# Early-fusion transformer on one core: when VectorE copies turned weights in the elastic attention, and how the expert weights are folded

## Chip, cores and metric

One NeuronCore of a Trainium2 chip runs the whole network in one launch. The metric is the device time in microseconds of one execution. All data are f32 in this part of the kernel; a matmul of f32 is issued as two passes, so that the trace shows two weight loads and two matmul records for each.

## What is computed

16 samples have 141 tokens each (64 image patches and 77 text tokens) of 192 features. A patch embedding is followed by two layers. The change touches the first layer's feed-forward block, which has an attention of its own, and a preparation for the second layer's experts.

```python
# first layer, "ffn": x [16, 141, 192]; large half (samples 0-7) and small half (8-15)
nl, ns = ln(x[:8]), ln(x[8:])
attn(xp, keep): q, k, v of 12 heads of 16; softmax(q k^T * scale) v; @ w_proj + b_proj
x = x + concat(attn(nl, all heads), sum_i gumbel[i] * attn(ns, 12 / (1, 2, 3) heads))
x = x + mlp(ln(x)), the small half with three widths of the input (192, 96, 64 features)

# second layer, attention of 4 experts
for e in range(4):
    o_e = windowed_attention_e(x)            # 12 heads of 16
    outs.append(o_e @ wo[e].T)
fused = concat(outs)
gate, value = silu(fused @ w_gate.T), fused @ w_up.T
```

Since nothing stands between `wo[e]` and the gate and up weights, the kernel multiplies them together once: for each expert a product of 192 x 192 by 192 x 384, called the fold.

## The kernel before, in words

The work is written out by hand for each engine. Every engine has its own program, run in order, and waits on semaphores. TensorE multiplies and turns, VectorE and ScalarE read its results out of the eight PSUM banks, GpSimd (POOL) scales the softmax weights and normalises tiles, SyncE issues DMAs.

**Elastic attention** (the loops `for n in range(B + 2)` of the four engines, B = 16). Iteration n scores sample n and finishes sample n - 1. TensorE's order in iteration n is: turn groups 0 and 1 of sample n - 1 (L1258), the scores of sample n into banks 0 to 3 (L1244) and of the 13 tail tokens of all heads into bank 7 (L1251), turn groups 2 and 3 (L1258), the V product of sample n into bank 6 (L1232), turn groups 4 and 5 (L1258), turn the tail rows (L1266), the output product of sample n - 2 (L1294), transposes of finished tiles (L700 to L706), the attended values of sample n - 1 (L1279), the q and k products of sample n + 2 (L505). A group is the softmax weights of four heads for one half of the keys, turned; the even groups go through bank 4 and the odd ones through bank 5, so that group u waits until group u - 2 has been copied out. ScalarE copies groups 0, 1 and 4 (L1370), VectorE groups 2, 3 and 5 (L1446).

ScalarE's order in iteration n is: copies of groups 0 and 1, the k copies (L497, L499), exponentials of bank 0, of the tail and of bank 1 (L1389, L1396), the copy of group 4, the tail copies (L1378, L1381), exponentials of banks 2 and 3, the evacuation of a turned tile (L711, L714). Each exponential is recorded as two instructions. Exponentials wait for the negated maxima that VectorE takes: L1425 for bank 0 and for bank 1, L1432 for the tail, and L1435 for banks 2 and 3 in one instruction.

VectorE's order in iteration n is: q of sample n + 1 (L482 to L489), `maxima(n)` with L1425, L1432, L1425, L1435, copies of groups 2 and 3 (L1446), copies of V (L1453), reciprocals of the sums (L1441, L1485), the copy of group 5, a residual addition, more reciprocals, the finish of sample n - 2 (L1468), statistics, and the copies of the attended values (L1462). POOL multiplies the weights by the reciprocals (L1506, L1519) for the turns of the next iteration.

**Fold.** It stands in the MLP block, between the first layer's first up product and the second: `up(0)`, `fold_products`, `up(1)`, `wide_down(0)`, and so on. `up_all(g)` (L1532) multiplies 384 tokens into banks 0 to 5, first six matmuls of 128 rows, then six of 64 rows that lie in the upper and the lower half of the array in turn; ScalarE's gelus (L1650) empty the banks. `fold_products` (L568) makes two products for each expert, of 128 and of 64 output rows, each from a chunk of 128 and a chunk of 64 contracted rows. They go to banks 6 and 7 in turn; ScalarE copies each out (L577, L580) into `gu_w0` and `gu_w1`. `up(1)` waits for all eight copies in its middle, ahead of three forward transposes (L705, L706) into banks 6 and 7, whose inputs POOL makes (L695). POOL then adds the residual tiles (L1725, L1728).

**Loads.** `load_late` on SyncE loads the weights of the MLP and of the fold once the first normalisation is through, and then waits (L552's issues) until the first attention has ended before it loads the experts' weights. The fold's inputs lie in a buffer of hidden values that is not used before the second up product.

Of the kernel before, what the change touches and what calls it, by code (L numbers as in the profile page):

```python
# [24 lines left out]
P = 128  # L25
C = 192
C1 = C - P
# [10 lines left out]
NH, HD, HP = 12, 16, 32  # L38
HB = NH // 4
EXPERTS = 4  # L40
# [21 lines left out]
def fusion_kernel(nc: bass.Bass, d: dict, out: bass.AP):  # L62
    with ExitStack() as ctx:
# [477 lines left out]
        def load_late(sp):  # L541
# [3 lines left out]
            for e in range(EXPERTS):  # L545
                sp.dma_start(eo[:, e, :, :].rearrange("p c (h x) -> p (c h) x", x=HD),
                             d["e_o"][e].rearrange("p c (h x) -> p (c h) x", x=HP)[:, :, 0:HD]).then_inc(w_fold, 16)
            sp.dma_start(eg[:, :, :], d["e_gu"].rearrange("e p c n -> p e (c n)")).then_inc(w_fold, 16)
# [10 lines left out]

        def fold_products(pe):  # L560
            pe.wait_ge(w_fold, 16 * (EXPERTS + 1))
            for e in range(EXPERTS):
                for b, rows_b in CH:
                    u = e * 2 + b
                    if u >= 2:
                        pe.wait_ge(s_c, u - 1)
                    for c, n in CH:
                        mm = nc.tensor.matmul(bank[6 + u % 2][0:rows_b, 0:2 * C],  # L568
                                              eo[0:n, e, c, b * P:b * P + rows_b],
                                              eg[0:n, e, c * 2 * C:(c + 1) * 2 * C],  # L570
                                              start=(c == 0), stop=(c == 1))
                    mm.then_inc(s_f, 1)

        def fold_evacuate(act):
            for e in range(EXPERTS):
                act.wait_ge(s_f, 2 * e + 1)
                nc.scalar.copy(gu_w0[:, e, :], bank[6][:, 0:2 * C]).then_inc(s_c, 1)  # L577
                act.wait_ge(s_f, 2 * e + 2)
                lo = e % 2 * C1
                nc.scalar.copy(gu_w1[lo:lo + C1, e // 2, :], bank[7][0:C1, 0:2 * C]).then_inc(s_c, 1)  # L580
# [27 lines left out]
        with ExitStack() as ph:  # L608
# [204 lines left out]
            with nc.Block() as block:  # L813
# [609 lines left out]
                def _(dve):  # L1423
# [4 lines left out]
                    def maxima(n):  # L1428
# [5 lines left out]
                        maximum(1)  # L1434
                        nc.vector.tensor_reduce(MX[:, 6:12].rearrange("p (i x) -> p i x", i=2),  # L1435
# [36 lines left out]
                    for n in range(B + 2):  # L1472
# [9 lines left out]
                        if n < B:  # L1482
                            evacuate_v(n)
# [45 lines left out]
                def _(pe):  # L1529
# [6 lines left out]
                    def up_all(g):  # L1536

                        pe.wait_ge(s_nev, T3 + min(3 * g + 3, IN_F))
                        for m in range(HM):
                            if m_first[g] + m >= 6:  # L1540
                                pe.wait_ge(s_mgl, m_first[g] + m - 5)
                            elif m == 4:
                                pe.wait_ge(s_nra, T3 + BACK_F)
                                pe.wait_ge(s_nev, T3 + IN_F)
                                pe.wait_ge(sf_o, 2 * B)
                            up_part(g, m, m, 0, 0, P, True, False)
# [822 lines left out]
```

## Time and profile before

| | us |
|---|---|
| median of 3 runs | 1101.53 (1101.25 to 1103.44) |
| the profiled execution | 1101.19 |
| its span, first to last instruction | 1099.5 |
| TensorE busy | 1062.5 |
| ScalarE busy | 763.4 |
| VectorE busy | 722.5 |
| POOL busy | 570.6 |

The span is what the trace sees; 1.7 us of the execution lie around it. Times in the rows are from the span's start. PE is a matmul on TensorE, PEld a weight load, DVE is VectorE, ACT is ScalarE, SP is SyncE. A row of a timeline gives the start, the duration, the engine, the line, the operation, output and input and the count; in brackets stands how long the engine was idle before it and which instruction of another engine ended that ("issue": none that the trace shows). Ends of matmuls are modelled, so a merged group may seem to overlap the next by 0.1 us.

### The profile page before, as it was taken

The page shows a single profiled execution, that of the slowest core. Times are in us where ns is not written, and L with a number is a line of the kernel's source. Part 1 is how long each engine was busy: PE and PEld are TensorE (multiplying, and loading weights), DVE is VectorE, ACT ScalarE, POOL GpSimd, SP SyncE. Part 2 cuts the span into 40 slices and gives each one's busy share as a digit, 9 for nine tenths or more (in the row PEclk, how much of TensorE's full clock was granted, in tenths as well). Part 3 has the DMA queues.
Part 4 walks back from the last instruction along what each step waited for, and adds up shares of the span by engine and source line. Part 5 has one row for each costly group of instructions (what it writes and reads, how often), then busy time and mean ns, then how long its engine had stood idle before and what let it go on. Part 6 is the DMA issues. An engine that isn't in the chain of part 4 may idle for free.

```text
span 1099.5 us, 34055 instructions
## 1 busy us (share of the span) xinstructions
PE 1062.5 (97%) x13103; PEld 864.5 (79%) x13103; DVE 722.5 (66%) x2256; ACT 763.4 (69%) x3370; POOL 570.6 (52%) x859
## 2 busy tenths in 40 slices
PE   6999998999999999999999999999999999999998
PEld 4788886777777475358888888888888888888677
DVE  8666567667766214367888878887888888887201
ACT  2356557777777435549988889888888888888231
POOL 2156766454455677436655465564465565566200
PEclk9999999999999999999999999999999999999999
DMA  8100603000000000010000000000000000000001
GB/s 275 30 6 1 137 2 76 6 2 1 2 1 1 1 1 1 1 52 3 2 3 3 3 2 3 3 3 3 3 2 2 3 2 3 3 2 3 11 22 33
DMA packets 35056, 19.66 MB, mean 18 GB/s; under 512 B 24656, under 2 KB 32336, under 8 KB 34896
## 3 DMA queue, kind: packets, MB, share of 16 engines
q1 hardware_dynamic: 34752, 17.00, 5.9%
q8 instruction: 105, 1.72, 0.7%
q14 instruction: 55, 0.45, 0.1%
q10 hardware_dynamic: 144, 0.49, 0.1%
HBM read 14.93 MB, written 1.77 MB: 15 GB/s over the span
## 4 chain that ended last, share of the span: by engine, by line
PE 89%; DVE 6%; ACT 3%; issue 1%; POOL 1%; DMA 1%; SPq 0%; DVEq 0%; POOLq 0%
PE banks L1750 8%; PE banks L1821 8%; PE banks L1758 6%; PE banks L1837 5%; PE banks L1532 5%; PE banks L1809 4%; PE banks L1856 4%; PE banks L2202 3%; PE banks L2156 3%; PE banks L1814 3%; PE banks L1258 2%; PE banks L505 2%; PE banks L1861 2%; PE banks L1279 2%; PE banks L1797 2%; PE banks L1844 2%
## 5 line engine op out<-in xcount | busy, mean ns | idle before, releaser
L2123 POOL TENSOR_TENSOR e_W<-e_W,e_RS 128x384 f32<-128x384 f32 x256 | 205.2, 828 | 231.7 <-DVE e_RS L1997 229.6
L1947 ACT ACTIVATE e_W<-banks,e_MX 128x128 f32<-128x128 f32 x768 | 270.1, 371 | 16.7 <-DVE e_MX L1983 16.6
L1947 ACT ACTIVATION_READ_ACCUMULATOR e_W<-banks,e_MX 128x1 f32 x768 | 161.2, 210 | 0.0
L1750 PE MATMUL banks<-XT,e_wqk 64*128 64x141 f32 x744 | 119.2, 295 | 0.0
L1750 PEld LDWEIGHTS banks<-XT,e_wqk 64*128 64x128 f32 x744 | 96.3, 188 | 18.1 <-issue 16.6
L1758 PE MATMUL banks<-e_wv,XT 128*128 128x192 f32 (+3 forms) x512 | 109.9, 344 | 0.6 <-DVE e_PT L2001 0.6
L1821 PE MATMUL banks<-ident,e_W 128*128 128x128 f32 x768 | 105.5, 273 | 1.2 <-POOL e_W L2123 0.8
L1506 POOL TENSOR_TENSOR f_W<-f_W,e_RS 128x423 f32<-128x423 f32 x64 | 56.3, 892 | 86.8 <-DVE e_RST L1485 76.5
L1941 ACT COPY e_PT<-banks 128x512 f32<-128x512 f32 x128 | 68.8, 589 | 40.5 <-PE banks L1821 40.3
L1983 DVE TENSOR_REDUCE e_MX<-banks 128x3 f32<-128x384 f32 x128 | 65.4, 552 | 40.1 <-PE banks L1809 40.1
L1821 PEld LDWEIGHTS banks<-ident,e_W 128*128 128x128 f32 x768 | 87.2, 143 | 2.4 <-DVE e_V L2010 1.0
L1758 PEld LDWEIGHTS banks<-e_wv,XT 128*128 128x128 f32 (+3 forms) x512 | 72.1, 166 | 4.6 <-DVE e_PT L2001 0.8
L1389 ACT ACTIVATE f_W<-banks,e_MX 128x141 f32<-128x141 f32 x192 | 70.2, 394 | 2.7 <-DVE e_MX L1425 2.0
L1837 PE MATMUL banks<-e_PT,e_V 128*32 128x128 f32 x1536 | 68.7, 277 | 0.0
L1809 PE MATMUL banks<-e_K,e_Q 32*128 32x128 f32 x1536 | 62.4, 285 | 0.0
L1258 PE MATMUL banks<-ident,f_W 128*70 128x128 f32 (+1 forms) x384 | 51.6, 276 | 10.3 <-DVE f_PT L1446 8.0
L1650 ACT ACTIVATE m_hid<-banks,vecs 128x384 f32<-128x384 f32 x72 | 38.1, 580 | 33.3 <-PE banks L1532 33.3
L1532 PE MATMUL banks<-XT,m_w 128*128 128x384 f32 (+1 forms) x216 | 60.8, 512 | 0.0
L1989 DVE TENSOR_REDUCE e_MX<-banks 128x6 f32<-128x768 f32 x64 | 60.6, 948 | 0.0
L1837 PEld LDWEIGHTS banks<-e_PT,e_V 128*32 128x32 f32 x1536 | 51.6, 109 | 9.2 <-issue 0.5
L1856 PE MATMUL banks<-e_ON,e_guw 128*128 128x141 f32 x384 | 57.9, 287 | 0.3 <-DVE e_ON L2022 0.3
L1258 PEld LDWEIGHTS banks<-ident,f_W 128*70 128x70 f32 (+1 forms) x384 | 40.7, 128 | 18.2 <-issue 14.9
(328 smaller groups left out, 2716.1 us busy)
## 6 DMA issues: line engine op xcount, KB each, us to landing
xp<-in_patches_dram SPq DMA_DIRECT2D x4, 768.0 KB, 9.3
H<-in_h_dram SPq DMA_DIRECT2D x1, 1728.0 KB, 13.4
out_dram<-H SPq DMA_DIRECT2D x6, 288.0 KB, 2.3
m_hid<-in_e_gu_dram SPq DMA_DIRECT2D x1, 1536.0 KB, 8.4
m_hid<-in_e_o_dram SPq DMA_DIRECT2D x4, 192.0 KB, 6.9
e_wqk<-in_e_qk_dram SPq DMA_DIRECT2D x8, 96.0 KB, 2.4
e_wqk<-in_e_qk_dram SPq DMA_DIRECT2D x24, 32.0 KB, 2.3
tokw<-in_tok_w_dram SPq DMA_DIRECT2D x1, 576.0 KB, 5.3
```

What stands on the lines that cost most here:

```text
L1258: tr = nc.tensor.transpose(bank[4 + u % 2][0:nk, x * P:(x + 1) * P], f_W[n % 2][:, u // 2 * 4 + x, k0:k0 + nk], ident[:, :])
L1389: ex = nc.scalar.activation(f_W[n % 2][:, t, :], bank[i][:, x * SEQ:(x + 1) * SEQ], ACT.Exp, bias=MX[:, t:t + 1], accum_out=SM[n % 2][:, t ...
L1532: return nc.tensor.matmul(bank[u % 6][:, 0:GT_], m_w1[lo:lo + n, c, m * P:(m + 1) * P], XT[lo:lo + n, c, g * GT_:(g + 1) * GT_], start=sta ...
L1750: return nc.tensor.matmul(bank[6][:, m * SEQ:(m + 1) * SEQ], ew[n % EXPERTS][0][0:rows_c, c, m * P:(m + 1) * P], XT[0:rows_c, c, tokens(n) ...
L1758: return nc.tensor.matmul(bank[4][0:nk, i * C:(i + 1) * C], XT[lo:P, c, at:at + nk], ew[n % EXPERTS][1][lo:P, c, :], start=start, stop=sto ...
L1809: mm = nc.tensor.matmul(bank[i][:, x * P:(x + 1) * P], QE[n % 2][HP * i:HP * (i + 1), q, :], KM[n % 2][HP * i:HP * (i + 1), k, 0:P], start ...
L1821: tr = nc.tensor.transpose(dst[:, (t % 4) * P:(t % 4 + 1) * P], W[n % 2][:, t, :], ident[:, :])
L1837: nc.tensor.matmul(bank[5][HP * c:HP * (c + 1), col:col + P], VP[n % 2][:, 0, h, :], PT[:, slot_of[h], :], start=(c not in seen), stop=(h ...
L1856: mm = nc.tensor.matmul(bank[7][:, m * SEQ:(m + 1) * SEQ], gu_w0[:, e, m * P:(m + 1) * P], ON[:, 0, :], start=(e == 0 and m == 0), stop=False,
L1941: nc.scalar.copy(PT[:, 4 * u:4 * u + 4, :], bank[4 + u][:, 0:4 * P]).then_inc(s_pa, 1)
L1947: ex = nc.scalar.activation(W[n % 2][:, t, :], bank[i][:, x * P:(x + 1) * P], ACT.Exp, bias=MX[:, t:t + 1], accum_out=SM[n % 2][:, t:t + 1])
L2123: nc.gpsimd.tensor_tensor(x, x, RS[n % 2][:, 3 * i:3 * i + 3].unsqueeze(2).broadcast_to([P, 3, P]), ALU.mult).then_inc(s_nm, 1)
```

## The change

In the elastic attention `maxima(n)` loses its last reduction, which becomes `last_maxima()` and is called behind the copies of groups 2 and 3 and ahead of the V copies. In the fold two experts are treated at once. The 64-row chunk of an odd expert is loaded to partitions 64 to 127, and its products of 64 output rows are written to partitions 64 to 127, so that the four kinds of product are issued in pairs: two full ones, two in the row halves, two in the column halves, two on the diagonal. The eight results have a bank each, of which banks 0 to 5 need the gelus' semaphore; `up_all(1)` waits for the copies bank by bank. Five DMAs become sixteen, which leave the padding out.

```diff
@@ load_late
             for e in range(EXPERTS):
-                sp.dma_start(eo[:, e, :, :].rearrange("p c (h x) -> p (c h) x", x=HD),
-                             d["e_o"][e].rearrange("p c (h x) -> p (c h) x", x=HP)[:, :, 0:HD]).then_inc(w_fold, 16)
-            sp.dma_start(eg[:, :, :], d["e_gu"].rearrange("e p c n -> p e (c n)")).then_inc(w_fold, 16)
+                lo = e % 2 * C1
+                for c, at, n in ((0, 0, P), (1, lo, C1)):
+                    sp.dma_start(eo[at:at + n, e, c, :].rearrange("p (h x) -> p h x", x=HD),
+                                 d["e_o"][e][0:n, c, :].rearrange("p (h x) -> p h x", x=HP)[:, :, 0:HD]).then_inc(w_fold, 16)
+                    sp.dma_start(eg[at:at + n, e, c * 2 * C:(c + 1) * 2 * C], d["e_gu"][e][0:n, c, :]).then_inc(w_fold, 16)
@@ the fold
+        FOLD_BANKS = ((6, 7, 0, 1), (2, 3, 4, 5))
+
+        def fold_part(dst, e, c, b, rows_b, start, stop):
+            lo, n = (e % 2 * C1, C1) if c else (0, P)
+            at = e % 2 * C1 if b else 0
+            return nc.tensor.matmul(dst[at:at + rows_b, 0:2 * C], eo[lo:lo + n, e, c, b * P:b * P + rows_b],
+                                    eg[lo:lo + n, e, c * 2 * C:(c + 1) * 2 * C], start=start, stop=stop,
+                                    tile_position=(lo, at), skip_group_check=True)
+
         def fold_products(pe):
-            pe.wait_ge(w_fold, 16 * (EXPERTS + 1))
-            for e in range(EXPERTS):
+            pe.wait_ge(w_fold, 16 * 4 * EXPERTS)
+            for q in range(EXPERTS // 2):
                 for b, rows_b in CH:
-                    u = e * 2 + b
-                    if u >= 2:
-                        pe.wait_ge(s_c, u - 1)
-                    for c, n in CH:
-                        mm = nc.tensor.matmul(bank[6 + u % 2][0:rows_b, 0:2 * C],
-                                              eo[0:n, e, c, b * P:b * P + rows_b],
-                                              eg[0:n, e, c * 2 * C:(c + 1) * 2 * C],
-                                              start=(c == 0), stop=(c == 1))
-                    mm.then_inc(s_f, 1)
+                    if (q, b) != (0, 0):
+                        pe.wait_ge(s_mgl, 4 * q + 2 * b)
+                    for c in range(2):
+                        for x in range(2):
+                            mm = fold_part(bank[FOLD_BANKS[q][2 * b + x]], 2 * q + x, c, b, rows_b, c == 0, c == 1)
+                            if c:
+                                mm.then_inc(s_f, 1)
 
         def fold_evacuate(act):
-            for e in range(EXPERTS):
-                act.wait_ge(s_f, 2 * e + 1)
-                nc.scalar.copy(gu_w0[:, e, :], bank[6][:, 0:2 * C]).then_inc(s_c, 1)
-                act.wait_ge(s_f, 2 * e + 2)
-                lo = e % 2 * C1
-                nc.scalar.copy(gu_w1[lo:lo + C1, e // 2, :], bank[7][0:C1, 0:2 * C]).then_inc(s_c, 1)
+            for q in range(EXPERTS // 2):
+                for x in range(2):
+                    act.wait_ge(s_f, 4 * q + x + 1)
+                    nc.scalar.copy(gu_w0[:, 2 * q + x, :], bank[FOLD_BANKS[q][x]][:, 0:2 * C]).then_inc(s_c, 1)
+                for x in range(2):
+                    act.wait_ge(s_f, 4 * q + x + 3)
+                    lo = x * C1
+                    nc.scalar.copy(gu_w1[lo:lo + C1, q, :], bank[FOLD_BANKS[q][2 + x]][lo:lo + C1, 0:2 * C]).then_inc(s_c, 1)
@@ elastic attention, VectorE
                         maximum(1)
+
+                    def last_maxima():
                         nc.vector.tensor_reduce(MX[:, 6:12].rearrange("p (i x) -> p i x", i=2),
...
                             evacuate_weights(n - 1, 3)
                         if n < B:
+                            last_maxima()
                             evacuate_v(n)
@@ up_all, TensorE
+                            if g == 1:
+                                pe.wait_ge(s_c, (4, 4, 5, 6, 8, 8)[m])
                             up_part(g, m, m, 0, 0, P, True, False)
```

## Rows read from the trace of the kernel before

**Rows 1.** The profile's page: the span, and the engines of the chain.

```profile
span 1099.5 us, 34055 instructions
...
PE 89%; DVE 6%; ACT 3%; issue 1%; POOL 1%; DMA 1%; SPq 0%; DVEq 0%; POOLq 0%
```

**Rows 2.** Windows (elastic attention, fold): length, busy PE, PEld, DVE, ACT, POOL, then clock.

```profile
174.00:366.00 192.00, 178.18 (x2107) 144.83 (x2108) 127.59 (x377) 142.89 (x626) 97.49 (x133) 1.00 0.05 10
372.87:385.89 13.02, 13.02 (x34) 3.88 (x32) 0.00 (x0) 5.08 (x11) 12.14 (x21) 1.00 0.00 0
```

**Rows 3.** The chain in order of time, iteration 8: start, duration, what.

```profile
262.32 0.94 DVE e_MX L1435
...
274.53 0.95 DVE e_MX L1435
```

**Rows 4.** Timeline of all engines in the same iteration 8.

```profile
261.17 1.04 PE L1258 MATMUL banks<-ident,f_W 128*71 128x128 f32 x8
...
262.04 1.46 PE L1232 MATMUL banks<-f_wv,XT 128*71 128x192 f32 x8
...
263.18 1.27 DVE L1446 COPY f_PT<-banks 71x512 f32<-71x512 f32 x2
...
264.01 1.13 PE L1258 MATMUL banks<-ident,f_W 128*71 128x128 f32 x8 [0.51 <-DVE f_PT L1446]
...
264.67 0.58 ACT L1370 COPY f_PT<-banks 71x512 f32<-71x512 f32 x1 [0.32 <-PE banks L1258]
...
265.31 0.58 PE L1266 MATMUL banks<-ident,f_WT 104*71 104x104 f32 x4 [0.17 <-ACT f_PT L1370]
...
266.39 0.40 ACT L1389 ACTIVATE f_W<-banks,e_MX 128x141 f32<-128x141 f32 x1
```

**Rows 5.** Waits of PE and of ACT, 178 to 345 us; then iteration 1's copy.

```profile
PE banks L1258 <- DVE f_PT L1446: 7.1, 14, 0.5
...
ACT f_PT L1370 <- PE banks L1258: 27.3, 28, 2.5
...
180.64 0.58 ACT L1370 COPY f_PT<-banks 71x512 f32<-71x512 f32 x1 [0.32 <-PE banks L1258]
```

**Rows 6.** Timeline of the fold: weight loads and one copy.

```profile
372.87 0.30 PEld L568 LDWEIGHTS banks<-m_hid 128*128 128x128 f32 x2 [0.55 <-issue]
373.71 0.29 PEld L568 LDWEIGHTS banks<-m_hid 64*128 64x128 f32 x2 [0.55 <-issue]
374.55 0.19 PEld L568 LDWEIGHTS banks<-m_hid 128*64 128x64 f32 x2 [0.55 <-issue]
375.34 0.19 PEld L568 LDWEIGHTS banks<-m_hid 64*64 64x64 f32 x2 [0.60 <-issue]
376.12 0.30 PEld L568 LDWEIGHTS banks<-m_hid 128*128 128x128 f32 x2 [0.60 <-issue]
...
376.23 0.47 ACT L580 COPY e_guw<-banks 64x384 f32<-64x384 f32 x1 [1.10 <-PE banks L568]
```

**Rows 7.** Timeline: a run of full matmuls, a run of row halves, column halves.

```profile
366.14 4.04 PE L1532 MATMUL banks<-XT,m_w 128*128 128x384 f32 x12
...
370.68 1.64 PEld L1532 LDWEIGHTS banks<-XT,m_w 64*128 64x128 f32 x12
...
446.34 0.20 PEld L1618 LDWEIGHTS banks<-m_hid,m_w 128*64 128x64 f32 x4 [0.62 <-issue]
447.14 0.16 PEld L1613 LDWEIGHTS banks<-m_hid,m_w 128*32 128x32 f32 x8 [0.60 <-issue]
```

**Rows 8.** Around the fold: gelus, POOL's last tiles, forward transposes, SyncE's wait.

```profile
371.68 2.94 ACT L1650 ACTIVATE m_hid<-banks,vecs 128x384 f32<-128x384 f32 x6 [2.78 <-PE banks L1532]
...
377.92 2.00 POOL L695 TENSOR_SCALAR f_xn<-XN,mv,rstd 128x192 f32<-128x192 f32 x2
...
389.87 0.27 PE L705 MATMUL banks<-ident,f_xn 128*128 128x128 f32 x1
...
SPq L552 <- DVE AT L1165: 40.8, 1, 40.8
```

## The prediction

> **What bounds the kernel now.** The page comes first: of a span of 1099.5 us, TensorE holds 89% of the chain that ended last [rows 1]. So an edit is worth what it takes out of TensorE's own stream of work and waits, and a microsecond spared on another engine counts only as far as TensorE was standing still for it. The windows come next: in the elastic attention's main stretch TensorE is busy 178.18 of 192.00 us, so it has gaps; in the fold it is busy for all of 13.02 us at full clock, while 32 weight loads, two for each of only 16 matmuls, stand there [rows 2]. The changed lines lie in exactly these two stretches. Then the chain in order of time shows, in one iteration (n = 8), the wide reduction L1435 (0.94) on the way to a VectorE copy, four transposes L1258 and a ScalarE copy L1370 [rows 3]. A reader could take it that 0.94 us per iteration stands to be won. The timeline of all engines corrects that: beside the reductions TensorE did eight transposes (261.17 for 1.04 us) and the V product (262.04 for 1.46 us), and it stood still only 0.51 us before the transposes at 264.01; ScalarE stood still only 0.32 us before its copy at 264.67 [rows 4]. These two idle times, not the 0.94, bound the gain.
>
> **Part 1, the order on VectorE.** Nothing is added or removed: in iterations 1 to 15 the reduction of twelve heads' last six maxima (L1435) goes from ahead of the copies of groups 2 and 3 (L1446, 1.27 us the two) to behind them. I follow one iteration. Maximum 1 ends at 262.32, where L1435 started [rows 3]. The eight transposes that fill both groups have been issued since 261.17 and end near 262.2 [rows 4], so the copies don't wait; they run 262.32 to 263.6. TensorE finishes the V product at about 263.5 (262.04 + 1.46), finds the first copy done (262.95), and starts groups 4 and 5 at 263.50 in place of 264.01; group 4 is full near 264.1. But the ScalarE copy of group 4 (L1370) is queued behind the exponentials of banks 0 and 1, which end 0.32 us ahead of its present start, at 264.35 [rows 4]. ScalarE is therefore late next: its copy moves from 264.67 to 264.35, the tail transposes L1266 that wait for it from 265.31 to 264.99, and all that follows on TensorE (it then runs to the next iteration without a wait for another engine). **Gain 0.32 us per iteration**; of TensorE's 0.51 us the rest turns into a longer wait ahead of L1266.
>
> What pays for it: the last maxima now run from 263.6 to 264.55. Queued behind them on VectorE are the V copies, two reciprocals and the copy of group 5. The order changes, their total does not, so that the V copies end where they ended, and so does the group 5 copy; the attend that needs it (L1279) comes on TensorE behind the tail transposes, the output product and the tile transposes. Exponentials 2 and 3 need the last maxima; they start at 266.39 [rows 4], in the changed kernel at 266.07, 1.5 us after the maxima. POOL's normalisations hang on the same reciprocals at the same time. So the move costs nothing while this 1.5 us stands.
>
> The wait of 0.5 us on TensorE occurs 14 times in the 14 iterations of the steady stretch, 7.1 us in all, and ScalarE's two kinds of waits at L1370 are 28 in 27.3 us, with the same 0.32 in the first iteration [rows 5] as in the eighth. Iteration 0 has no copies and iteration 16 no maxima: 15 x 0.32 = **4.8 us**. Bounds: nothing if the copy ended up where it was; 15 x 0.51 = 7.7 us if TensorE got back its whole wait, for which ScalarE would have to be free earlier; a loss is in the last rival. I take the ScalarE row's value, because that engine has no slack ahead of it.
>
> **Part 2, the fold's matmuls.** Before: 16 matmuls in 13.02 us [rows 2]. Their weight loads start at 372.87, 373.71, 374.55, 375.34 and 376.12, so 0.84, 0.84, 0.79 and 0.78 us each, and each load waits 0.55 to 0.60 us for no other engine [rows 6]. The four matmuls of an expert use 128x128, 64x128, 128x64 and 64x64 of the array, so the form changes with each one. Where the form stays the same it is faster: six 128x128 matmuls of 384 columns take 4.04 us, 0.67 each [rows 7]. Where tiles lie in different halves they run together: six matmuls with 64 rows in alternating halves fill 370.68 to 372.87, 2.19 us, so with 0.67 for each pair that follows in a run, a pair alone is 2.19 - 1.34 = 0.85; a pair of 128x64 in two column halves takes 446.34 to 447.14, 0.80 us [rows 7].
>
> After, for two experts: two full matmuls 0.84 + 0.67 = 1.51; a pair in row halves 0.85; a pair in column halves 0.80; a pair of 64x64 on the diagonal, which no row shows, between 0.78 (one alone [rows 6], if they run fully together) and 0.78 + 0.67 (one after the other), taken at 0.80 by the column pair, its nearest row. Sum 3.96, for four experts 7.92. **13.02 - 7.92 = 5.1 us.** Bounds: if no pair runs together, 1.51 + 1.51 + 2 x 1.46 (0.79 + 0.67) = 5.94 per two experts, 11.9 in all, a gain of 1.1; if the changes of form cost nothing, 10 x 0.67 = 6.7, a gain of 6.3.
>
> What hangs on it: the evacuations stay eight ScalarE copies of some 0.48 us [rows 6], now two by two. The last two can start only with the end of the fold and take 1.0 us; the following up product (L1532) needs bank 4 after four of its matmuls, 2.7 us later, so the new waits on s_c don't stop it. The new waits on gelus 2, 4 and 6 are met: all six gelus end by 374.62 (371.68 + 2.94), and the first bank beyond 6 and 7 is written near 375.2 [rows 8]. The forward transposes of the last tiles move from 389.87 to about 384.8; POOL's normalised tiles for them are ready at 379.92 [rows 8], 4.9 us of cover. The vectors that add the residual follow TensorE and are not late.
>
> DMAs: 5 issues become 16, with the padding left out. They stand ahead of SyncE's wait for the attention, where the queue idles 40.8 us [rows 8], and nobody reads them before 372.87. At most 16 issues lengthen a queue that is idle: 0.
>
> **Sum.** Against the profiled execution's 1101.19 us (span 1099.5 and 1.7 around it; the median of the runs shown, 1101.53, is 0.3 above): 1101.2 - 4.8 - 5.1 = **1091.3 us**. What such a measurement can tell from no change is about 0.2%, 2.2 us.
>
> **Rivals.**
> 1. *The pairs don't run together* (a semaphore increment on each closing matmul, or two banks written at once): the fold takes 11.9, the time is 1101.2 - 4.8 - 1.1 = 1095.3. For it: no row has a diagonal pair. Against: the row and column pairs of [rows 7], of the same width. 0.10.
> 2. *Only tiles in different rows overlap.* A load would then be ahead of a running matmul only where the rows differ: the second full matmul costs 0.84 and the column pair 2 x 0.79, so 1.68 + 0.85 + 1.58 + 0.80 = 4.91 per two experts, 9.8 in all, a gain of 3.2, the time 1093.2. Against it: 0.67 for full matmuls in a run, and the column pair at 0.80 [rows 7]. 0.05. The Trainium skill (TensorE: Matmul & The Clock Gate, Part 3, The mechanism) states this rule, that loads overlap running matmuls only when the row group differs; here the trace speaks against it.
> 3. *Part 1 is hidden.* The tail transposes start where they did, since something else of that moment ends last: 1101.2 - 5.1 = 1096.1. For it: TensorE, VectorE and ScalarE all change hands within 1.3 us here. Against: ScalarE's wait names the transposes. 0.07.
> 4. *Part 1 gives TensorE's whole 0.51 us*: 1101.2 - 7.7 - 5.1 = 1088.4. It needs ScalarE's exponentials to end 0.2 us sooner, and nothing moves these. 0.09.
> 5. *Both weak* (1 and 3): 1101.2 - 1.1 = 1100.1, within 0.2%. 0.04.
> 6. *Slower: the last maxima come late.* The copy of group 3 waits for transposes that wait for POOL's third normalisation, and the last maxima stand behind it; once they end after 266.07 they hold exponentials 2 and 3, with them ScalarE and TensorE's next iteration. The cover is 1.5 us. A copy held up by 2.5 us would start the exponentials at 267.05 and not at 266.39: 15 x 0.66 = 9.9 lost, 5.1 won, 1106.0. It decides from 2.2 us of delay on. For it: the transposes end only 0.1 us ahead of the first copy. Against: they are already issued at 261.17 without a wait. 0.03.
>
> **Numbers.** The forecast has 0.62. The range reaches from rival 4's side to rival 1, 1088.3 to 1095.4, and leaves out 3, 5 and 6 (0.14). Faster by over 0.2%: 0.62 + 0.10 + 0.05 + 0.07 + 0.09 = 0.93; same 0.04; slower 0.03.
>
> **What would show it.** In the changed profile: the iteration is 11.9 us in place of 12.21 (from L1435 at 262.32 to the next at 274.53 [rows 3]); TensorE's wait for VectorE at L1258 is gone in 15 iterations and its wait for ScalarE at L1266 grows from 0.17 to about 0.45; ScalarE has no idle time before the copy of group 4; the exponentials of banks 2 and 3 wait for nothing. The fold holds TensorE for 7.9 us, weight loads come in groups of four, and the first up matmuls behind it wait for no ScalarE copy. I am wrong if ScalarE waits for L1435's reduction, if the fold is over 9 us, or if TensorE waits between the fold and the experts' first scores where it did not.

## The result, and the profile of the changed kernel

| | before | changed |
|---|---|---|
| median, us | 1102.49 (1101.25 to 1104.81, 4 runs) | 1091.95 (1089.48 to 1092.55, 4 runs) |
| profiled execution, us | 1101.19 | 1089.48 |
| its span, us | 1099.5 | 1087.7 |
| first elastic scores to the fold's first load, us | 206.01 | 199.52 |
| the fold's first to the next product's first load, us | 13.02 | 7.84 |
| first elastic scores to the end of the span, us | 932.64 | 920.87 |

The ratio of the times, taken against runs of the kernel before on the same chip, is 0.9892 [0.9871, 0.9913], faster by 1.1%; the two medians of the table alone would give 0.9904. The two profiled executions lie 11.8 us apart, the medians 10.5. The forecast was 1091.3 us; the two terms of its sum came out at 6.49 us (forecast 4.8) and 5.18 us (forecast 5.1). Everything behind the fold lasts as long as before: from its end to the end of the span 713.6 us before and 713.5 after.

The stretch ahead of the first elastic scores, at about 167 us, holds none of the change and varies by up to 8.5 us between the profiled executions of this document, mostly for a reason that the last section shows. So the parts are compared from the first scores on.

The changed kernel's page, its span and chain, answers to [rows 1]:

```profile
span 1087.7 us, 34071 instructions
...
PE 88%; ACT 7%; DVE 3%; POOL 1%; issue 1%; DMA 1%; SPq 0%; DVEq 0%; POOLq 0%
```

TensorE nearly keeps its share (89% before, 88% now). VectorE's went from 6% to 3% and ScalarE's from 3% to 7%: in the elastic attention a part of the path has passed from VectorE to ScalarE. The chain in order of time shows it, one iteration (start, duration, what), where [rows 3] had L1435 twice:

```profile
257.79 0.61 DVE e_MX L1436
...
258.43 1.19 ACT f_W L1400 x6
259.62 0.72 ACT f_WT L1407 x4
260.34 1.08 ACT f_W L1400 x6
261.42 0.46 ACT f_PT L1381
...
261.92 0.58 PE banks L1277 x4
...
273.68 0.58 PE banks L1277 x4
```

Lines have moved by about 11: L1400 is the exponential (L1389 before), L1407 that of the tail, L1381 ScalarE's copy of turned weights (L1370), L1269 the transposes (L1258), L1277 those of the tail (L1266), L1448 the last maxima (L1435), L1459 VectorE's copies (L1446). An iteration, tail transposes to tail transposes, is 273.68 - 261.92 = 11.76 us, where it was 12.21. These are steady iterations: most of those in the middle of the loop have this length, while a few, and those at both ends, have other waits and other lengths. The timeline of all engines in the iteration before it, which answers to [rows 4] (brackets: idle before, and who ended it):

```profile
247.34 1.46 PE L1243 MATMUL banks<-f_wv,XT 128*71 128x192 f32 x8
...
247.54 1.27 DVE L1459 COPY f_PT<-banks 71x512 f32<-71x512 f32 x2
...
248.64 1.04 PE L1269 MATMUL banks<-ident,f_W 128*71 128x128 f32 x8
...
248.73 1.02 DVE L1448 TENSOR_REDUCE e_MX<-banks 128x6 f32<-128x846 f32 x1
...
249.42 0.24 ACT L1400 ACTIVATION_READ_ACCUMULATOR f_W<-banks,e_MX 128x1 f32 x1
249.51 0.59 ACT L1381 COPY f_PT<-banks 71x512 f32<-71x512 f32 x1
...
250.16 0.58 PE L1277 MATMUL banks<-ident,f_WT 104*71 104x104 f32 x4 [0.48 <-ACT f_PT L1381]
...
251.24 0.40 ACT L1400 ACTIVATE f_W<-banks,e_MX 128x141 f32<-128x141 f32 x1
```

VectorE's copies lie ahead of the wide reduction; the transposes L1269 start without a wait, 1.30 us behind the V product (L1243, L1232 before) where it was 1.97 (264.01 - 262.04 in [rows 4]); ScalarE's copy has no idle time before it, and TensorE now waits for ScalarE, 0.48 us before L1277. The waits between 178 and 345 us (engine, line, waited for; total us, times, longest), which answer to [rows 5], say the same of all iterations; no wait of the L1269 transposes for VectorE is left among them:

```profile
ACT f_PT L1381 <- PE banks L1269: 23.0, 14, 2.5
...
PE banks L1277 <- ACT f_PT L1381: 7.3, 15, 0.5
```

ScalarE's waits at its copies went from 28 ([rows 5]) to 14: the wait ahead of group 4 is gone, the one ahead of group 0 stays.

The fold's weight loads, which answer to [rows 6]:

```profile
366.35 0.94 PEld L567 LDWEIGHTS banks<-m_hid 128*128 128x128 f32 x4 [0.55 <-issue]
367.83 0.30 PEld L567 LDWEIGHTS banks<-m_hid 64*128 64x128 f32 x4 [0.55 <-issue]
368.68 0.20 PEld L567 LDWEIGHTS banks<-m_hid 128*64 128x64 f32 x4 [0.55 <-ACT m_hid L1666]
369.47 0.20 PEld L567 LDWEIGHTS banks<-m_hid 64*64 64x64 f32 x4 [0.60 <-issue]
370.27 0.94 PEld L567 LDWEIGHTS banks<-m_hid 128*128 128x128 f32 x4 [0.60 <-issue]
...
374.19 1.26 PEld L1546 LDWEIGHTS banks<-XT,m_w 128*128 128x128 f32 x5 [0.60 <-issue]
```

A row here stands for the four weight loads of a pair. The steps from one row to the next are 1.48, 0.85, 0.79 and 0.80 us: the full pair, the row pair, the column pair and the diagonal pair. A gelu is named at 368.68, but the idle time there is the same 0.55 as everywhere, so that wait was met.

### The profile page after: what moved, and what is told of

Same layout as the page of the kernel before. It is cut to its first block, busy times and chain, and to the rows that moved or that the text cites. A ratio compares the mean times of both kernels' runs of the same rounds, so it can differ in the third digit from the quotient of the medians.

```text
span 1087.7 us, 34071 instructions
## 1 busy us (share of the span) xinstructions
PE 1053.4 (97%) x13103; PEld 865.2 (80%) x13103; DVE 720.6 (66%) x2256; ACT 762.3 (70%) x3370; POOL 572.7 (53%) x859
## 4 chain that ended last, share of the span: by engine, by line
PE 88%; ACT 7%; DVE 3%; POOL 1%; issue 1%; DMA 1%; SPq 0%; DVEq 0%; POOLq 0%
PE banks L1766 8%; PE banks L1837 8%; PE banks L1774 6%; PE banks L1853 5%; PE banks L1546 5%; PE banks L1825 4%; PE banks L1872 4%; ACT f_W L1400 4%; PE banks L2218 3%; PE banks L2172 3%; PE banks L1830 3%; PE banks L505 2%; PE banks L1877 2%; PE banks L1290 2%; PE banks L1813 2%; PE banks L1860 2%
## 5 line engine op out<-in xcount | busy, mean ns | idle before, releaser
L1400 ACT ACTIVATE f_W<-banks,e_MX 128x141 f32<-128x141 f32 x192 | 70.3, 394 | 2.8 <-DVE e_MX L1436 2.2
L1269 PE MATMUL banks<-ident,f_W 128*70 128x128 f32 (+1 forms) x384 | 50.1, 273 | 2.8 <-POOL f_W L1520 1.1
L1546 PEld LDWEIGHTS banks<-XT,m_w 128*128 128x128 f32 (+1 forms) x216 | 27.9, 188 | 28.9 <-issue 12.3
```

The lines of the kernel that those rows point to most:

```text
L1400: ex = nc.scalar.activation(f_W[n % 2][:, t, :], bank[i][:, x * SEQ:(x + 1) * SEQ], ACT.Exp, bias=MX[:, t:t + 1], accum_out=SM[n % 2][:, t ...
L1546: return nc.tensor.matmul(bank[u % 6][:, 0:GT_], m_w1[lo:lo + n, c, m * P:(m + 1) * P], XT[lo:lo + n, c, g * GT_:(g + 1) * GT_], start=sta ...
```

## The experiments

All times "from the first scores" are of the one profiled execution of each kernel, first elastic scores to the end of the span, and are set against the 932.64 us of before or the 920.87 us of the change. The medians come with their runs; ratios are to the kernel before on the same chip. Where an expectation names theories A and B, these are rival explanations with the time that each would give.

| kernel | median (runs) | ratio | from the first scores | to before |
|---|---|---|---|---|
| changed | 1091.95 (4) | 0.9892 [0.9871, 0.9913] | 920.87 | -11.77 |
| order_only | 1097.38 (6) | 0.994 [0.9922, 0.9959] | 925.99 | -6.65 |
| fold_only | 1096.68 (7) | 0.9948 [0.9926, 0.9969] | 927.39 | -5.25 |
| fold_unpaired | 1095.3 (6) | 0.9925 [0.9908, 0.9942] | 925.94 | -6.70 |
| fold_by_form | 1090.58 (5) | 0.9876 [0.9856, 0.9897] | 920.05 | -12.59 |
| one_copy_ahead | 1094.13 (6) | 0.9915 [0.9894, 0.9936] | 921.85 | -10.79 |
| maxima_late | 1092.89 (6) | 0.9916 [0.9897, 0.9935] | 923.21 | -9.43 |
| tail_in_gap | 1092.83 (6) | 0.9913 [0.9892, 0.9933] | 923.47 | -9.17 |
| tail_in_gap_by_form | 1093.59 (6) | 0.9915 [0.9895, 0.9936] | 922.77 | -9.87 |
| one_exp_in_gap | 1089.31 (4) | 0.9879 [0.986, 0.9897] | 917.42 | -15.22 |
| one_exp_in_gap_by_form | 1088.65 (6) | 0.987 [0.9848, 0.9892] | 916.66 | -15.98 |
| changed_again | 1092.78 (4) | 0.9905 [0.9889, 0.9921] | 922.06 | -10.58 |

### The two parts by themselves

order_only is the kernel before with the move on VectorE alone. fold_only is the changed kernel with that move undone:

```diff
                         maximum(1)
-
-                    def last_maxima():
                         nc.vector.tensor_reduce(MX[:, 6:12].rearrange("p (i x) -> p i x", i=2),
...
                         if n < B:
-                            last_maxima()
                             evacuate_v(n)
```

> The kernel before with the new order on VectorE alone. Theory A, read from the changed kernel's trace: each of 15 iterations gains 0.45 us, 0.32 of ScalarE's wait and 0.13 because a ScalarE copy that is already queued starts inside its predecessor's accumulator read; iteration 11.76 us, time 6.5 to 6.8 below the kernel before. Theory B, as predicted: 0.32 each, iteration 11.89, 4.8 below. The fold stays at 13.02 us.

> The kernel before with the new fold alone. Both theories: iteration 12.21 us as before, fold 7.84 us, time 5.2 below the kernel before. If the two parts help or hinder each other, this gain and that of the order alone do not add up to the 11.8 us between the two profiled spans.

order_only gained 6.65 us, its elastic stretch is 199.38 us against 206.01, its iteration 11.76 us and its fold 13.03. fold_only gained 5.25 us: its fold is 7.84 us and its elastic stretch, 205.99, that of before. 6.65 + 5.25 = 11.90 against the 11.77 of both together: the parts add up, and the order alone gives what theory A had (11.76 us, 6.5 to 6.8), not the prediction's 4.8. fold_only's timeline has the idle times of [rows 4] back, with VectorE's copies (L1457 there) behind the reduction:

```profile
251.83 1.14 PE L1269 MATMUL banks<-ident,f_W 128*71 128x128 f32 x8 [0.51 <-DVE f_PT L1457]
...
252.49 0.58 ACT L1381 COPY f_PT<-banks 71x512 f32<-71x512 f32 x1 [0.32 <-PE banks L1269]
...
253.13 0.58 PE L1277 MATMUL banks<-ident,f_WT 104*71 104x104 f32 x4 [0.16 <-ACT f_PT L1381]
```

### What gives the fold its time

The changed fold differs from the one before in two things, the places of its tiles (other banks, other halves, sixteen DMAs) and the order in which they are issued. fold_unpaired keeps the places and puts each expert's tiles back behind one another; fold_by_form goes the other way and treats all four experts at once (the copies and their waits follow in the same order):

```diff
-                    for c in range(2):
-                        for x in range(2):
+                    for x in range(2):
+                        for c in range(2):
```

```diff
-            for q in range(EXPERTS // 2):
-                for b, rows_b in CH:
-                    if (q, b) != (0, 0):
-                        pe.wait_ge(s_mgl, 4 * q + 2 * b)
-                    for c in range(2):
-                        for x in range(2):
-                            mm = fold_part(bank[FOLD_BANKS[q][2 * b + x]], 2 * q + x, c, b, rows_b, c == 0, c == 1)
+            for b, rows_b in CH:
+                for c in range(2):
+                    for e in range(EXPERTS):
+                        if c == 0 and e == 2 * (1 - b):
+                            pe.wait_ge(s_mgl, 2 + 4 * b)
+                        mm = fold_part(bank[FOLD_BANKS[b][e]], e, c, b, rows_b, c == 0, c == 1)
```

> The changed kernel, but in the fold each product's two chunks follow one another (expert by expert), so that no two matmuls of one form are neighbours; banks, semaphores, halves and loads stay as changed. Theory A (neighbours of one form are what counts): the fold takes 13.0 us again, 5.2 more than the changed kernel. Theory B (the eight banks and the missing wait for ScalarE's copies are a part of the gain): the fold stays below 11 us.

> The changed kernel, but all four experts of one form of product stand together: four full matmuls, two pairs in row halves, two in column halves, two on the diagonal, so 4 changes of form and not 8. Theory A: a change costs some 0.15 to 0.2 us, the fold takes 7.84 - 4 x 0.17 = 7.15 us, time 0.7 below the changed kernel. Theory B (what costs is the pair's own start, not the change): 7.8 us as before.

fold_unpaired's loads, with the other banks, halves and DMAs in place:

```profile
366.75 0.30 PEld L567 LDWEIGHTS banks<-m_hid 128*128 128x128 f32 x2 [0.55 <-issue]
367.59 0.29 PEld L567 LDWEIGHTS banks<-m_hid 64*128 64x128 f32 x2 [0.55 <-issue]
...
372.47 0.19 PEld L567 LDWEIGHTS banks<-m_hid 64*64 64x64 f32 x2 [0.60 <-issue]
...
379.77 0.30 PEld L1546 LDWEIGHTS banks<-XT,m_w 128*128 128x128 f32 x2 [0.60 <-issue]
```

Each matmul again costs 0.84 or 0.79 us, and the fold is 13.02 us, exactly that of before. So the new places give nothing in the old order: the gain comes only once tiles of one form stand beside each other. Whether the new order would give a part of it in the old places was not tested; there the 64-row and 64-column tiles of two experts would share a half of the array, and [rows 7] shows tiles running together only in different halves. fold_by_form's loads:

```profile
370.12 2.23 PEld L567 LDWEIGHTS banks<-m_hid 128*128 128x128 f32 x8 [0.55 <-issue]
372.89 0.95 PEld L567 LDWEIGHTS banks<-m_hid 64*128 64x128 f32 x8 [0.55 <-issue]
374.38 0.20 PEld L567 LDWEIGHTS banks<-m_hid 128*64 128x64 f32 x4 [0.54 <-issue]
...
375.82 0.20 PEld L567 LDWEIGHTS banks<-m_hid 64*64 64x64 f32 x4 [0.60 <-issue]
...
377.26 2.88 PEld L1544 LDWEIGHTS banks<-XT,m_w 128*128 128x128 f32 x10 [0.60 <-issue]
```

The fold takes 377.26 - 370.12 = 7.14 us: the four full matmuls 2.77 (2 x 1.48 in pairs), two row pairs 1.49 (2 x 0.85), two column pairs 1.44 (2 x 0.79), two diagonal pairs 1.44 (2 x 0.80). Four changes of form fewer save 0.70 us, 0.17 us each, in the trace; from the first scores it is 0.82. The medians, 1090.58 against 1091.95, are too close to show it. The Trainium skill (TensorEngine Tiling (Array Packing), Key Properties) says that a change of tiling mode drains TensorE; this trace agrees and puts the price here at 0.14 us (column pairs, 2 x 0.79 - 1.44) to 0.21 (row pairs, 2 x 0.85 - 1.49).

### Where the last maxima may stand

one_copy_ahead puts them behind the first of the two copies. maxima_late puts them behind the V copies, the reciprocals and the copy of group 5, which gives exponentials 2 and 3 a late start, as the prediction's last rival had it:

```diff
                             evacuate_weights(n - 1, 2)
-                            evacuate_weights(n - 1, 3)
                         if n < B:
                             last_maxima()
+                        if 1 <= n <= B:
+                            evacuate_weights(n - 1, 3)
+                        if n < B:
                             evacuate_v(n)
```

```diff
                         if n < B:
-                            last_maxima()
                             evacuate_v(n)
...
                             evacuate_weights(n - 1, 5)
+                        if n < B:
+                            last_maxima()
```

> The changed kernel, but with the last maxima between VectorE's copies of groups 2 and 3 (only the copy of group 2 is ahead of them). Theory A (TensorE's group 4 and with it ScalarE's queue need only the copy of group 2): ScalarE still has no idle time before its copy of group 4, but TensorE's group 5 waits for the copy of group 3, ends near the moment at which the tail transposes could start or 0.3 us after it, and the iteration is 11.8 to 12.05 us instead of 11.76, time 1 to 4 us above the changed kernel. Theory B (both copies must be ahead): 12.21 us, 6.5 above.

> The changed kernel, but with the last maxima behind the V copies, the reciprocals and the copy of group 5 as well, so that they end about 0.4 us after the moment at which ScalarE could start exponentials 2 and 3. The pricing of the last rival in the prediction: each such delay goes to the time, 15 x 0.4 = 6 us more. Theory A (ScalarE waits 1.7 us for TensorE at the head of each iteration and takes the delay up there): iteration 11.76 us, time within 1 us of the changed kernel; only the last two iterations, where no q and k product follows, may lose 0.4 each.

one_copy_ahead, the timeline of TensorE and ScalarE:

```profile
252.89 0.60 PE L1269 MATMUL banks<-ident,f_W 128*71 128x128 f32 x4
...
253.77 0.59 ACT L1381 COPY f_PT<-banks 71x512 f32<-71x512 f32 x1
...
254.07 0.63 PE L1269 MATMUL banks<-ident,f_W 128*70 128x128 f32 x4 [0.58 <-DVE f_PT L1459]
254.53 0.52 PE L1277 MATMUL banks<-ident,f_WT 104*71 104x104 f32 x4
```

Group 4's transposes start in time, so ScalarE's copy has no idle time; group 5's now wait 0.58 us for VectorE, and the tail transposes start 0.76 us behind the copy and not 0.65. The iteration is 11.83 us, as theory A had it. So the copy of group 2 alone releases nearly the whole gain, and that of group 3 is worth 0.07 us per iteration (15 x 0.07 = 1.05; from the first scores it is 0.98 slower than the change).

maxima_late, the timeline:

```profile
251.94 0.59 ACT L1381 COPY f_PT<-banks 71x512 f32<-71x512 f32 x1
...
252.85 1.02 DVE L1448 TENSOR_REDUCE e_MX<-banks 128x6 f32<-128x846 f32 x1
```

The reduction now ends at 253.87, 1.93 us behind the copy's start. Exponentials 2 and 3 start at 253.91, 1.97 us behind it and not 1.73 as in the change (251.24 - 249.51), so they are 0.24 us late. Still the steady iteration is 11.76 us, as in the change. The kernel loses 2.34 us against the change all the same, more than the 1 us of theory A, and 2.28 of it in the elastic stretch (201.80 us against 199.52). Up to iteration 1's tail transposes it loses 1.83, because in iteration 0 ScalarE has no copies to do and waits for the maxima:

```profile
174.50 0.38 ACT L1400 ACTIVATE f_W<-banks,e_MX 128x141 f32<-128x141 f32 x1 [1.23 <-DVE e_MX L1448]
```

Iteration 2 gives 0.25 back. Iterations 12, 15 and 16 lose 0.23, 0.24 and 0.24: there TensorE's first transposes wait for ScalarE's evacuation of a turned tile (L725), 0.66 us in place of 0.43 in the last two, so ScalarE's delay reaches TensorE. In the steady iterations ScalarE waits 1.49 us at the head of the next iteration for the first transposes anyway, 0.24 less than the change's 1.73, and that wait takes up the delay.

### ScalarE as the new limit: two attempts

TensorE waits 0.48 us for ScalarE's copy of group 4, whose input is full near 249.3 (an estimate: where the copy has to wait, in fold_only, it starts 0.66 us behind its transposes, here at 248.64) while ScalarE still has exponentials ahead of it. Work that stands ahead of the copy and isn't urgent could go behind it, into the time in which ScalarE waits for the tail transposes (0.67 us). tail_in_gap moves both exponentials of the tail there, with the reciprocals that depend on them and the wait of the output product for bank 7; one_exp_in_gap moves only the last of bank 1's three:

```diff
                             exponentials(n, 0)
-                            exponentials_tail(n)
                             exponentials(n, 1)
...
                             evacuate_weights(n - 1, 4)
+                        if n < B:
+                            exponentials_tail(n)
+                        if 1 <= n <= B:
                             evacuate_tail(n - 1)
...
-                        pe.wait_ge(sf_ex, 5 * min(n + 2, B - 1) + 2)
+                        pe.wait_ge(sf_ex, 5 * min(n + 2, B - 1) + 3)
```

```diff
                             exponentials_tail(n)
-                            exponentials(n, 1)
+                            exponentials(n, 1, (0, 1))
                         if 1 <= n <= B:
                             evacuate_weights(n - 1, 4)
+                        if n < B:
+                            exponentials(n, 1, (2,))
+                        if 1 <= n <= B:
                             evacuate_tail(n - 1)
```

The two kernels named by_form add fold_by_form's order to these.

> The changed kernel, but ScalarE takes exponentials 1 and the copy of group 4 ahead of the tail's exponentials, which then fill its 0.67 us of waiting for the tail transposes; the tail's reciprocals move behind VectorE's copy of group 5. Theory A (ScalarE's queue ahead of the copy of group 4 is the bound now): the copy starts when group 4 is full, 0.2 to 0.3 us sooner, the tail transposes follow, iteration 11.5 to 11.65 us, time 2 to 4 us below the changed kernel. Theory B (TensorE's transposes and the output product, which now waits for the tail's exponentials, are the bound): 11.7 us or more, no gain.

> The kernel with the tail's exponentials in ScalarE's gap and, besides, the fold with all four experts of one form together. The two edits lie in different stretches: the fold takes 7.15 us and the iteration what it takes with the first edit alone, so that the time is 0.7 us below that kernel.

> The changed kernel, but ScalarE takes the third of bank 1's exponentials behind the copy of group 4, in the gap in which it waits for the tail transposes; the output product doesn't wait for it. Theory A (ScalarE's queue bounds the changed iteration; a reorder fails only where TensorE gets a new wait, as the output product did on the tail's exponentials): group 4 is full about 0.3 us ahead of the copy's present start, so the copy starts 0.2 to 0.3 us sooner and the iteration is 11.45 to 11.6 us, 3 to 4.5 us in all. Theory B: the copy then waits for TensorE again and loses the 0.13 to 0.15 us of overlap with its predecessor, so that only 0.15 us or less remain, iteration 11.6 to 11.7. Theory C (TensorE's own instructions fill the rest): no gain.

> The kernel with the third exponential of bank 1 in the gap and, besides, the fold with all four experts of one form together: the fold 7.15 us, the iteration as with the first edit alone, the time 0.7 us below that kernel and 1.5 to 5 us below the changed kernel.

tail_in_gap, the timeline:

```profile
251.02 1.04 PE L1269 MATMUL banks<-ident,f_W 128*71 128x128 f32 x8
251.66 0.58 ACT L1381 COPY f_PT<-banks 71x512 f32<-71x512 f32 x1 [0.34 <-PE banks L1269]
252.29 0.58 PE L1277 MATMUL banks<-ident,f_WT 104*71 104x104 f32 x4 [0.23 <-ACT f_PT L1381]
...
253.11 1.35 PE L1305 MATMUL banks<-f_ON,f_wp 128*128 128x141 f32 x8 [0.24 <-ACT f_WT L1407]
```

Theory B came. ScalarE is now early and waits for the transposes, and TensorE gets a new wait of 0.24 us ahead of the output product L1305, since bank 7 must be read out first. From the start of the V product to that of the tail transposes TensorE needs 0.25 us less than in the change, but the output product starts 0.82 us behind the tail transposes (253.11 - 252.29) and not 0.41, so that the new wait costs 0.41 us and not the 0.24 in brackets. The iteration is 11.97 us, 0.21 more than the change's, and the kernel loses 2.60 us against it. tail_in_gap_by_form is 0.70 us better than tail_in_gap from the first scores, which is the fold's part, though its median is not the lower one.

one_exp_in_gap, the timeline:

```profile
248.11 1.04 PE L1269 MATMUL banks<-ident,f_W 128*71 128x128 f32 x8
248.75 0.58 ACT L1381 COPY f_PT<-banks 71x512 f32<-71x512 f32 x1
249.39 0.58 PE L1277 MATMUL banks<-ident,f_WT 104*71 104x104 f32 x4 [0.23 <-ACT f_PT L1381]
249.80 1.29 PE L1305 MATMUL banks<-f_ON,f_wp 128*128 128x141 f32 x8
250.00 0.25 ACT L1389 COPY f_PT<-banks 71x104 f32<-71x104 f32 x1 [0.30 <-PE banks L1277]
```

Here the copy starts 0.64 us behind its transposes (0.87 in the change), without idle time; the output product doesn't wait and starts 0.41 us behind the tail transposes, as in the change; ScalarE's own wait ahead of the tail copies (L1389 here) falls to 0.30 us. The iteration is 11.51 us, 0.25 less than the change's, as theory A had it, and 3.45 us are won from the first scores (15 x 0.25 = 3.75). The two kernels differ in which exponentials move, in how many, and in whether TensorE's output product has to wait for them; the rows show the loss at that wait, and moving one of the tail's exponentials alone was not tried. With the fold by form, one_exp_in_gap_by_form is 916.66 us from the first scores, 4.21 less than the change, and its median 1088.65 us, ratio 0.987 [0.9848, 0.9892] to the kernel before: the lowest of all. On the same chip the changed kernel (changed_again, below) has a median of 1092.78 and 0.9905 [0.9889, 0.9921]. The intervals still overlap by a little, so that it beats the changed kernel is shown by the traces and only suggested by the medians.

### The changed kernel once more

> The changed kernel once more, on the same chip as the two beside it. From the first scores of the elastic attention to the end 920.9 us as in its first profile, within 0.3; the time before those scores may differ by some us from execution to execution.

It came out at 922.06 us from the first scores, 1.19 more than the first profile of the same kernel and outside the 0.3 expected. Its elastic stretch repeats within 0.15 us (199.37 and 199.52); the difference lies behind the fold (714.85 us against 713.5), where a window of 120 us, 367.01 to 487.01, shows a granted clock of 0.99 in place of 1.00 (the share of its full 2.4 GHz that TensorE was granted). So differences of about 1 us from the first scores are within what one kernel does by itself, and those of the fold (0.70) rest on the fold's own rows, which repeat to 0.01 us.

## Why the prediction was right, and which term was off

**What bounds the kernel.** The gain did come out of TensorE's own idle time: the wait of 0.51 us at L1258 went, in every steady iteration, and the 0.94 us of the reduction was not to be had. But the idle times of the rows, 0.51 on TensorE and 0.32 on ScalarE, were too small as bounds, as part 1 shows.

**Part 1.** The mechanism held: VectorE's copies no longer wait, TensorE starts early, ScalarE is late next, and TensorE's wait before the tail transposes grows (0.17 forecast to become 0.45, measured 0.48). The size was off. The step that failed is "its copy moves from 264.67 to 264.35", that is, that the copy can't start before the end of the exponential's second record. In the changed kernel it starts at 249.51, while that record runs from 249.42 to 249.66: 0.15 us ahead of its end. Where ScalarE had to wait, the copy started 0.56 us behind the record's start (264.67 - 264.11, the record 0.24 us long up to 264.35), where it doesn't, 0.09. That is 0.47 us, 0.45 in the length of the iteration, and not 0.32. In these rows a queued copy overlaps the record before it and one that has to wait does not, so the idle time in brackets is less than what is to be won.

The same holds on TensorE. Its transposes start 1.30 us behind the V product in place of 1.97, so the wait recorded as 0.51 us cost 0.67; the tail transposes start 1.52 us behind the transposes in place of 1.30 (250.16 - 248.64, 265.31 - 264.01), which takes 0.22 back and leaves 0.45. The sum over the loop, 15 x 0.45 = 6.75, is 6.49 in the trace, since iteration 2 gained only 0.20 (11.37 to 11.17 us). It lies between the stated bounds 0 and 7.7, but 15 x 0.51 = 7.7 was no true upper bound: 15 x 0.67 is 10.

**The rest of part 1.** The V copies, the reciprocals and POOL cost nothing, as forecast; exponentials 2 and 3 (251.24) start 1.49 us after the maxima end (249.75), the forecast cover of 1.5.

**Part 2.** All four kinds of pair were priced within 0.03 us: 1.51 forecast and 1.48 measured, 0.85 and 0.85, 0.80 and 0.79, and the diagonal pair, of which no row was there, 0.80 and 0.80. The forward transposes start 11.81 us behind the fold's start (forecast 11.9), still 4.7 us behind POOL's tiles, and no matmul behind the fold waits for a copy. The DMAs cost nothing that shows: the first scores start at 166.83 us (166.86 before), the fold's first load has the same 0.55 us of idle time ahead of it, and what lies behind the fold lasts as long as before. fold_unpaired shows besides that the new places without the new order gain nothing; the new order without the new places was not tried.

**The rivals.** The first two fell with the rows of the fold; the second by 0.64 us for the second full matmul (1.48 - 0.84) and 0.79 for the column pair. The Trainium skill (TensorE: Matmul & The Clock Gate, Part 3, The mechanism) names two ways for a load to get ahead of a running matmul, another row group or the background weight buffer, and then says that only the row group counts; the runs here contradict that narrower sentence twice. The third and the fifth fell with order_only. The fourth, TensorE's whole 0.51, came nearer than I thought: 0.45 us, without any exponential ending sooner. **The sixth was priced wrongly.** It let a late start of exponentials 2 and 3 lengthen each of 15 iterations by as much. maxima_late made them 0.24 us late and the steady iteration stayed at 11.76, since ScalarE waits 1.7 us for TensorE at the head of the next one; only iterations 12, 15 and 16 grew by it. That wait was there before, too (1.75 us with the old order, in fold_only), and I did not add it to the cover. The rival's own delay of 0.66 us is also below this slack, but no run has one that large, and how large a delay holds the steady loop up was not tried.

**The sum.** 4.8 + 5.1 = 9.9 was forecast; the trace shows 6.49 + 5.18 = 11.67. The median of 1091.95 is close to the forecast of 1091.3, but that is in part luck: it is 2.5 us above the profiled execution, and that execution missed the forecast by 1.8 us on the low side.

## What to carry to other kernels

The gain from a removed wait is not the length of what stood ahead of it but runs up to the next engine's queue: follow the wait to whoever is late next, and add what its queued instructions overlap, since the idle time recorded before an instruction was here less than what its removal brought (0.32 us recorded and 0.45 won, 0.51 recorded and 0.67 gone). Before pricing a delay on an engine, look for its slack over the whole iteration, not only at the place of the delay, and look at the first and last iterations by themselves. Small matmuls, as those of this fold, were cheapest sorted by the form of their tile, with tiles of different halves beside each other. Once a limit has moved to another engine, an instruction moved into its idle time gains only if no other engine gets a new wait for it.

## What the runs showed of the hardware that I had not expected

**ScalarE overlaps queued instructions.** A copy that doesn't wait starts 0.15 us ahead of the end of the accumulator's read before it (above); a copy that had to wait has lost that. On TensorE, too, a wait cost more than the idle time recorded for it: 0.67 us for 0.51 at the transposes, 0.41 us for 0.24 at tail_in_gap's output product.

**A change of form has a price of its own.** A matmul of 384 columns costs 0.84 us alone among others and 0.64 behind one of its own form; row, column and diagonal pairs of 64 cost 0.85, 0.79 and 0.80 alone and some 0.65 behind a pair of the same form (1.49 - 0.85, 1.44 - 0.79, 1.44 - 0.80).

**The clock can fall early in the program, while TensorE is busy.** Two kernels with the same instructions up to there, in windows of 4 us (length, busy PE, granted clock, DMA share, GB/s). First one_exp_in_gap, then one_exp_in_gap_by_form:

```profile
36.00:40.00 4.00, 4.00 (x21) 1.00 0.12 30
...
44.00:48.00 4.00, 4.00 (x29) 1.00 0.08 18
```

```profile
36.00:40.00 4.00, 4.00 (x17) 0.75 0.16 40
40.00:44.00 4.00, 4.00 (x13) 0.50 0.03 9
44.00:48.00 4.00, 4.00 (x15) 0.50 0.00 0
48.00:52.00 4.00, 4.00 (x25) 0.97 0.01 2
```

In the second, the granted clock goes from 1.00 (2.4 GHz) to 0.50 (1.2 GHz), by the 0.75 of the first window at about 38 us, and is back at about 48, though TensorE was busy without a break from 20 us on. Its first elastic scores start at 175.34 us and those of the first at 167.58. Three other profiled executions have shorter falls at the same place (0.77 and 0.81 in order_only's two windows, 0.59 in the first window of fold_by_form and one_copy_ahead) and start their first scores at 172.11, 170.74 and 170.74; the nine without a fall start them between 166.83 and 169.13. So these falls make up most of the spread ahead of the first scores. What sets off the fall stays open: the windows from 20 to 36 us read 4.00 us busy at a clock of 1.00 in both.
